# Layer 0's attention: rows normalised two tiles ahead and projected one slot ahead, weight remainders a slot later, and the first steps of the last feed-forward reordered

## The reference

```python
# layer 0, attention: 16 heads of 16; the query is the layer-normalised x
q = (query @ Wq + bq).reshape(B, Nq, H, D).transpose(0, 2, 1, 3)
k, v = (key_value @ Wk + bk), (key_value @ Wv + bv)        # split into heads likewise
attn = jnp.einsum('bhqd,bhkd->bhqk', q, k) * scale
attn = jnp.clip(attn, -CLAMP, CLAMP)
attn = jax.nn.softmax(attn, axis=-1)
x = jnp.einsum('bhqk,bhkd->bqhd', attn, v).reshape(B, Nq, Cq)
return x @ Wo + bo
...
# layer 1, feed-forward: rows and hidden values as 16-bit integers with one scale for the whole tensor
def quantize_a16(x):
    amax = jnp.clip(jnp.max(jnp.abs(x)), 1e-08, None)
    scale = 32767.0 / amax
    x_q = jnp.clip(jnp.round(x * scale), -32768.0, 32767.0) / scale
```

## Time and profile before

| what | us |
|---|---|
| median of three runs | 1161.29 |
| the profiled run's own time | 1163.3 |
| its span, first to last instruction | 1161.2 |
| TensorE (PE) busy | 1057.4 |
| VectorE (DVE) busy | 916.9 |
| ScalarE (ACT) busy | 834.7 |
| GpSimd (POOL) busy | 539.4 |
| layer 0's attention | 0 to about 246 |
| granted TensorE clock, mean | 0.975 |

### The profile page before, as it was taken

One profiled execution on the slowest core, in us unless ns is written; L12 is line 12 of the kernel. 1 busy time (PEld: TensorE's weight loads), 2 busy tenths in 40 slices (PEclk: granted clock), 3 DMA queues, 4 the chain that ended last, 5 costly groups with the idle time before them and its releaser, 6 DMA issues.

```text
span 1161.2 us, 26321 instructions
## 1 busy us (share of the span) xinstructions
PE 1057.4 (91%) x8919; PEld 775.3 (67%) x8919; DVE 916.9 (79%) x1960; ACT 834.7 (72%) x2382; POOL 539.4 (46%) x515
## 2 busy tenths in 40 slices
PE   6888888868969999999999999589999999889898
PEld 5666666645537777777777777357777777645477
DVE  5999999957845687666666667479999999789798
ACT  4988889836656456556556667378888888569896
POOL 5888888732252122122122111178889887500140
PEclk9999999979989999999999999889999999989899
DMA  6443334349672343333333335345252423010034
GB/s 150 118 128 110 110 110 133 123 128 284 189 206 61 53 137 90 118 101 121 124 104 120 121 115 161 112 127 161 68 158 67 154 74 92 28 38 0 1 119 137
DMA packets 128814, 132.12 MB, mean 114 GB/s; under 512 B 24792, under 2 KB 112973, under 8 KB 128557
## 3 DMA queue, kind: packets, MB, share of 16 engines
q1 hardware_dynamic: 119901, 112.17, 32.0%
q0 software_dynamic: 6480, 17.70, 5.5%
q10 hardware_dynamic: 2304, 0.59, 0.3%
HBM read 82.78 MB, written 47.64 MB: 112 GB/s over the span
## 4 chain that ended last, share of the span: by engine, by line
PE 57%; DVE 4%; ACT 4%; issue 2%; DMA 1%; POOL 1%; DVEq 0%; SPq 0%; ACTq 0%; POOLq 0%
PE exp_ps_h L1527 15%; PE exp_ps_y L1540 9%; PE a_ps_o L1953 9%; PE a_ps_sc L1937 8%; PE f_ps_h L2264 5%; PE exp_ps_y L1546 5%; PE a_ps_p L1924 3%; ACT exp_h L1590 2%; DVE f_hlo L2395 2%; PE exp_ps_x L1506 1%; PE f_ps L2447 1%; PE f_ps L2443 1%; PE f_ps_x L2255 1%; DVE all_xn L2404 1%; PE a_ps_x L1911 1%
## 5 line engine op out<-in xcount | busy, mean ns | idle before, releaser
L1590 ACT ACTIVATE exp_h<-exp_ps_h,exp_b_now 128x256 f32<-128x256 f32 (+1 forms) x320 | 124.7, 440 | 142.4 <-PE exp_ps_h L1527 142.4
L1491 POOL DMA_INDIRECT exp_xg<-xn,all_token_of x71 | 84.4, 1188 | 304.0 <-PE exp_ps_x L1506 288.5
L1527 PE MATMUL exp_ps_h<-exp_xhi,exp_w_now 128*128 128x256 bf16 (+1 forms) x1280 | 196.4, 263 | 5.9 <-DVE exp_xlo L1625 5.9
L1986 ACT ACTIVATE a_z<-a_ps_sc,a_nmx 128x77 f32<-128x77 f32 x512 | 159.3, 367 | 35.6 <-DVE a_nmx L2088 35.6
L1527 PE MATMUL exp_ps_h<-exp_xlo,exp_w_now 128*128 128x256 bf16 (+1 forms) x640 | 161.4, 263 | 0.0
L1703 DVE TENSOR_TENSOR exp_hlo<-exp_h,exp_hhi 128x512 bf16<-128x512 f32 (+1 forms) x160 | 99.4, 632 | 70.4 <-ACT exp_hhi L1597 68.5
L1540 PE MATMUL exp_ps_y<-moe_w2s,exp_hhi 128*128 x568 | 134.2, 379 | 1.3 <-DVE exp_y L1722 1.3
L1527 PEld LDWEIGHTS exp_ps_h<-exp_xhi,exp_w_now 128*128 128x128 bf16 x1280 | 120.6, 99 | 20.7 <-issue 8.3
L1986 ACT ACTIVATION_READ_ACCUMULATOR a_z<-a_ps_sc,a_nmx 128x1 f32 x512 | 127.0, 248 | 0.0
L1953 PE MATMUL a_ps_o<-a_v_now,a_phi 128*128 128x256 bf16 (+1 forms) x640 | 106.6, 272 | 2.3 <-DVE a_plo L2077 2.3
L1937 PE MATMUL a_ps_sc<-a_k_now,a_xhi 128*128 128x462 bf16 (+1 forms) x384 | 98.6, 341 | 3.4 <-DMA a_k_now<-fold_klo 2.2
(11 more groups left out here) (279 smaller groups left out, 2735.5 us busy)
## 6 DMA issues: line engine op xcount, KB each, us to landing
a_stage<-in_L_ffn_W_dram SPq DMA_DIRECT2D x64, 256.0 KB, 3.2
y_slots<-exp_y SPq DMA_DIRECT2D x71, 128.0 KB, 1.7
fold_k<-route_kst SPq DMA_DIRECT2D x16, 308.0 KB, 4.5
fold_v<-route_vst SPq DMA_DIRECT2D x16, 308.0 KB
exp_job_in<-fold_k SPq DMA_DIRECT2D x14, 352.0 KB, 3.3
exp_job_in<-fold_v SPq DMA_DIRECT2D x14, 352.0 KB, 3.3
a_x<-in_x_dram SPq DMA_DIRECT2D x32, 128.0 KB, 2.3
x<-a_xo SPq DMA_DIRECT2D x32, 128.0 KB, 1.7
```

What stands on the lines that cost most here:

```text
L1491: pool.indirect_dma_start(out=xg[:, v, u, :], out_offset=None, in_=xn_dram[:, :], in_offset=bass.IndirectOffsetOnAxis(ap=at.bitcast(U32), ...
L1527: mm = pe.matmul(hidden[:, i, f % 2, slots(j)], w1_now[:, v, k, hl, f * P:(f + 1) * P], xx[:, k, slots(j)], start=(q == 0), stop=(q == len ...
L1590: ins = act.activation(h[:, f, slots(j)], hidden[:, i, f % 2, slots(j)], ACT.Gelu_apprx_tanh, bias=b1_now[:, v, f:f + 1])
L1986: ins = act.activation(z[:, u, h * KEYS:(h + 1) * KEYS], ps_sc[:, j, (h - SB[j][0]) * KEYS:(h - SB[j][0] + 1) * KEYS], ACT.Exp, bias=nmx[: ...
```

## The change

In `attention`:

- ScalarE normalises the rows of tile T+2 in slot T (before: T+1), and copies the queries of T+1 (before: T). TensorE starts a slot with the turn of T+1's rows and projects T+1 in the middle of the slot. VectorE copies the turned rows ahead of the maxima. The residual comes after the maxima.
- GpSimd makes the weight remainders of piece T-1 in slot T, ahead of the normalisation of the weights (before: of piece T, one part ahead of and one behind it).
- TensorE's turns and values products alternate: first set of turns, output of T-3, queries of T+1, second set, products of the chunks 0 to 3, third set, products of the chunks 4 to 7, products of the chunks 8 and 9. Each set keeps the order of `turns` among its own.
- ScalarE copies the attended values of T-2 at the end of the slot (before: at the start of the next), and the high parts stand between the copies.
- In slot 0 and 1 the projections of values and keys stand in new places among these.

In `ffn`: the reciprocal of a scale and the per-column steps are computed after the first scaling; `magic` is set in the first phase; TensorE does two products of group 0 ahead of the turns of group 1; the second phase's engines wait for the steps by the first phase's semaphore.

The diff, cut:

```diff
@@ -158,6 +158,7 @@
       if q < ng * LANES and c * P < (q + 1) * PAIR and (c + 1) * P > q * PAIR]
 lanes = [[i for q in range(ng * j, ng * j + ng) for i, (c, qq, _) in enumerate(blocks) if qq == q] for j in range(LANES)]
 turns = [i for row in itertools.zip_longest(*lanes) for i in row if i is not None]
+part = [[i for i in turns if blocks[i][0] // 4 == k] for k in range(3)]
 scale = float(dh) ** -0.5
...
@@ -359,31 +360,32 @@
     def slot(T, t, b):
         u = t % 2
+        v = (t - 1) % 2
+        w1, w2 = split["w1s"], split["w2s"]
+        if has(T - 1):
+            pool.wait_ge(s["hi_done"], 2 * T - 1)
+            at, cols = (T - 1) // 2, slice(v * 512, (v + 1) * 512)
+            pool.tensor_tensor(w1[:, at, 1, cols], stage[:, v, 0, :], w1[:, at, 0, cols],
+                               ALU.subtract).then_inc(s["lo_done"], 1)
         if has(T + 2):
             power(T + 2, u)
+        if has(T - 1):
+            pool.wait_ge(s["hi_done"], 2 * T)
+            pool.tensor_tensor(w2[:, 2 * T - 2:2 * T, D:2 * D],
+                               stage[:, v, 1, :].rearrange("p (g d) -> p g d", d=D),
+                               w2[:, 2 * T - 2:2 * T, 0:D], ALU.subtract).then_inc(s["lo_done"], 1)
         if has(T):
             pool.wait_ge(s["xn_done"], T + 1)
             pool.tensor_tensor(x[:, t, :], x[:, t, :], gbo[:, :], ALU.add).then_inc(s["xb_done"], 1)
-            pool.wait_ge(s["hi_done"], 2 * T + 1)
-            w1, w2 = split["w1s"], split["w2s"]
-            at, cols = T // 2, slice(u * 512, (u + 1) * 512)
-            pool.tensor_tensor(w1[:, at, 1, cols], stage[:, u, 0, :], w1[:, at, 0, cols],
-                               ALU.subtract).then_inc(s["lo_done"], 1)
         if has(T - 1):
-            v = (t - 1) % 2
             pool.wait_ge(s["rsum_done"], T)
             zt = z[:, (T - 1) % NZ, :].rearrange("p (h k) -> p h k", k=KEYS)
             pool.tensor_tensor(zt, zt, rsum[:, v, :].unsqueeze(2).broadcast_to((P, HEADS, KEYS)),
                                ALU.mult).then_inc(s["norm_done"], 1)
-        if has(T):
-            pool.wait_ge(s["hi_done"], 2 * T + 2)
-            pool.tensor_tensor(w2[:, 2 * T:2 * T + 2, D:2 * D],
-                               stage[:, u, 1, :].rearrange("p (g d) -> p g d", d=D),
-                               w2[:, 2 * T:2 * T + 2, 0:D], ALU.subtract).then_inc(s["lo_done"], 1)
     run(pool, slot)
...
@@ -425,24 +426,41 @@
     pe.wait_ge(C.ctx_copied, 2 * B)
     pe.wait_ge(C.ones_row, 1)
     pe.wait_ge(keys_in, 16 * 3)
...
+    def attend(T, some):
+        for i in some:
+            c, q, half = blocks[i]
+            j, g = q // ng, q % ng
+            mine = [cc for cc, qq, _ in blocks if qq == q]
+            n = min(P, ROWS - c * P)
+            mm = pe.matmul(ps_v[32 * j:32 * j + 32, g * P:(g + 1) * P], vblk[0:n, T // TPB % 2, c, half, :], pT[0:n, c, :],
+                           start=(c == mine[0]), stop=(c == mine[-1]))
+        return mm
     keys(0, 1, 0)
     turn_x(0)
     pe.wait_ge(queries_in, 32)
+    queries(0)
     def slot(T, t, b):
...
+        if has(T + 1):
+            wait(pe, s["pT_done"], 3 * (T - 2))
+            pe.wait_ge(s["qT_done"], T + 1)
+            turn_x(T + 1)
         if has(T):
             pe.wait_ge(s["qT_done"], T + 1)
             if t == 0:
...
@@ -454,40 +472,37 @@
                     mm = pe.matmul(ps_sc[:, j, g * PAIR:(g + 1) * PAIR], qT[lane, g, :], kblk[lane, b % 2, g, :],
                                    start=True, stop=True)
             mm.then_inc(s["scores_done"], 1)
+        if T == 1:
+            values(1, 0)
         if has(T - 2):
-            pe.wait_ge(s["norm_done"], T - 1)
             if T == 2:
                 pe.wait_ge(s["kT_done"], 1)
-            for j in range(2):
-                wait(pe, s["pT_done"], 3 * (T - 3) + j + 1)
-                turn_p(T - 2, j)
-            pe.wait_ge(s["qT_done"], min(T + 1, TILES))
-            wait(pe, s["xnT_done"], min(T + 1, TILES))
+            pe.wait_ge(s["norm_done"], T - 1)
+            wait(pe, s["pT_done"], 3 * (T - 3) + 1)
+            turn_p(T - 2, 0)
+        if has(T - 3):
+            output(T - 3)
+        if has(T + 1):
+            queries(T + 1)
+        if has(T - 2):
+            wait(pe, s["pT_done"], 3 * (T - 3) + 2)
+            turn_p(T - 2, 1)
+            wait(pe, s["xo_done"], T - 2)
+            if t == 2:
+                pe.wait_ge(s["v_done"], (T - 2) // TPB + 1)
+            pe.wait_ge(s["pT_done"], 3 * (T - 2) + 1)
+            attend(T - 2, part[0])
+            pe.wait_ge(s["qT_done"], min(T + 2, TILES))
+            wait(pe, s["pT_done"], 3 * (T - 3) + 3)
             turn_p(T - 2, 2)
-        if has(T + 1):
-            turn_x(T + 1)
-        if has(T - 2):
-            wait(pe, s["xo_done"], T - 2)
...
+            pe.wait_ge(s["pT_done"], 3 * (T - 2) + 2)
+            attend(T - 2, part[1])
+            pe.wait_ge(s["pT_done"], 3 * (T - 2) + 3)
+            attend(T - 2, part[2]).then_inc(s["pv_done"], 1)
         if T == 0:
             pe.wait_ge(weights_in, 16 * N_WEIGHTS)
             values(0, 1)
         if T == 1:
-            values(1, 0)
             pe.wait_ge(s["v_rows_done"], 2)
             keys(1, B, 0)
...
-        if has(T - 3):
-            act.wait_ge(s["pv_done"], T - 2)
...
             act.activation(pT[:, 0:4, :].rearrange("p c t -> p (c t)"), ps_p[:, 0, :], ACT.Copy).then_inc(s["pT_done"], 1)
+        if has(T):
+            act.wait_ge(piece_in[u], 32 * (T // 2 + 1))
+            act.activation(split["w1s"][:, T // 2, 0, u * 512:(u + 1) * 512],
+                           stage[:, u, 0, :], ACT.Copy).then_inc(s["hi_done"], 1)
+        if has(T + 1):
+            short_queries(T + 1)
         if has(T - 2):
             act.wait_ge(s["turned_p"], 3 * (T - 2) + 2)
             act.activation(pT[:, 4:8, :].rearrange("p c t -> p (c t)"), ps_p[:, 1, :], ACT.Copy).then_inc(s["pT_done"], 1)
-        if has(T):
-            act.wait_ge(piece_in[u], 32 * (T // 2 + 1))
-            act.activation(split["w1s"][:, T // 2, 0, u * 512:(u + 1) * 512],
-                           stage[:, u, 0, :], ACT.Copy).then_inc(s["hi_done"], 1)
-        if has(T - 2):
             act.wait_ge(s["turned_p"], 3 * (T - 2) + 3)
-            act.wait_ge(s["xnT_done"], min(T + 2, TILES))
             act.activation(pT[:, RCH - 2:RCH, :].rearrange("p c t -> p (c t)"), ps_q, ACT.Copy).then_inc(s["pT_done"], 1)
         if has(T):
             act.activation(split["w2s"][:, 2 * T:2 * T + 2, 0:D],
                            stage[:, u, 1, :].rearrange("p (g d) -> p g d", d=D),
                            ACT.Copy).then_inc(s["hi_done"], 1)
+        if has(T + 2):
+            normal(T + 2, u, (t + 2) % RING)
+        if has(T - 2):
+            act.wait_ge(s["pv_done"], T - 1)
+            wait(act, s["o_done"], T - 2)
+            act.activation(attnT[:, :, :].rearrange("p g t -> p (g t)"), ps_v, ACT.Copy).then_inc(s["attn_done"], 1)
         if T == 0:
             v_copy(0)
         if T == 1:
-            v_copy(1)
             act.wait_ge(s["k_proj"], 2)
             act.activation(kT[:, :, 1:B, :].rearrange("p g b k -> p g (b k)"), ps_p[:, 0:ng, 0:(B - 1) * KEYS],
                            ACT.Copy).then_inc(s["kT_done"], 1)
@@ -653,12 +672,17 @@
             ln_stats(T + 2, u, (t + 2) % RING, b + (t + 2) // RING)
         if has(T + 2):
             ln_mean(T + 2, u)
+        if has(T + 1):
+            turned(T + 1)
         if T == 2:
             block_values(0)
         if t == 3 and b + 1 < B:
             block_keys(b + 1)
         if t == 5 and b + 1 < B:
             block_values(b + 1)
+        if has(T):
+            dve.wait_ge(s["scores_done"], T + 1)
+            dve.tensor_reduce(mx[:, :].rearrange("p (j x) -> p j x", j=LANES), scores, AX, ALU.max).then_inc(s["max_done"], 1)
         if has(T - SKEW):
             v = (t - SKEW) % 2
             turn = b if t >= SKEW else b - 1
@@ -669,11 +693,6 @@
             dve.scalar_tensor_tensor(out=xo[:, v, :], in0=ps_o, scalar=C.gate[:, gate_col:gate_col + 1],
                                      in1=x[:, (t - SKEW) % RING, :], op0=ALU.mult,
                                      op1=ALU.add).then_inc(s["xo_done"], 1)
-        if has(T):
-            dve.wait_ge(s["scores_done"], T + 1)
-            dve.tensor_reduce(mx[:, :].rearrange("p (j x) -> p j x", j=LANES), scores, AX, ALU.max).then_inc(s["max_done"], 1)
-        if has(T + 1):
-            turned(T + 1)
         if has(T + 2):
             ln_shift(T + 2, u)
         if has(T - 1):
...
-def steps_of(dve, sem, count, amax_all, out, tmp):
-    for ins in (lambda: dve.tensor_scalar(tmp[:, 0:1], amax_all[:, 0:1], 1e-8, None, ALU.max),
-                lambda: dve.reciprocal(tmp[:, 1:2], tmp[:, 0:1]),
-                lambda: dve.tensor_scalar(out[:, 0:1], tmp[:, 1:2], 32767.0, None, ALU.mult),
-                lambda: dve.reciprocal(out[:, 1:2], out[:, 0:1])):
-        ins().then_inc(sem, 1)
```

(33 more changed lines are left out.)

90 lines of the change are left out of this document (34 added, 56 removed).

## The result

The changed kernel takes 1163.55 us (median of 20 runs, 1161.00 to 1166.85), the kernel before 1160.99 (20 runs beside it): ratio 1.0022, 95% interval 1.0015 to 1.0028, so 2.6 us slower. I had forecast 1165.8, slower by 4.5. Side and range were right.

What follows compares the result with a forecast made beforehand. VectorE was taken to bound the kernel before (6.81 us a slot), TensorE the changed one (6.95). Slots +2.3, start +1.0, end +2.2 and last stage -1.0 gave +4.5: 1165.8 us, range 1153 to 1171.

Steps and rivals of the forecast that it cites:

- What bounds the kernel now: Layer 0's attention: VectorE sets the 6.81 us slot, 0.50 of it a clamp stall beside GpSimd; real need 6.31.
- Rival C: VectorE stays the bound in layer 0's attention, slots of 6.35 to 6.4, 1147 us; chance 0.12.
- Remainders at nothing: GpSimd's later weight remainders cost nothing and free the clamp (0.50 us); ScalarE stalling on a weight piece would contradict cover.
- The values product: TensorE in layer 0's attention: three parts take 0.88, 1.10 and 0.66, together 2.64 us, against 1.10 of pure work interleaved.
- Rival D: No overlap of TensorE's product parts, full price of passages: slots of 7.2, on average 7.25, 1173 us; chance 0.13.
- TensorE's sum: TensorE's work per changed attention slot: 7.03 to 7.23 us without overlap, 6.5 to 7.1 with it, taken as 6.95.
- Masks: Block masks on VectorE, one of 1.5 us in four slots, cost about 0.05 us a slot on average after the change.
- End: End of layer 0's attention: later output product, split products and later last ReLU, less VectorE's lead, together +2.2 us.
- Start: Start of layer 0's attention: value projections later, first value mask 1 to 1.5 us later, clamp gives 0.4 back: +1.0 us.
- Last stage: Feed-forward: first phase gains 0.34 us and 0.6 us, second phase gains nothing; together -1.0 us.
- A: The forecast case: TensorE bounds layer 0's attention at about 6.95 us a slot, 1163 to 1169 us; chance 0.45.
- B: Deep overlap of product parts two and three (their 20 instructions in 1.3 us): TensorE 6.6, 1155.7 to 1160; chance 0.30.

Runs made afterwards that it cites:

- remainders_later: The kernel before with only GpSimd's two weight remainders of piece T-1 taken in slot T: 1159.4 us, ratio 0.9969 to the kernel before.
- copies_rows_first: The changed kernel with the values product interleaved in one place, ScalarE's copies and rows moved earlier, GpSimd's first ffn scaling behind VectorE's: 1153.09 us, ratio 0.9918.
- together: The changed kernel with the values product as one interleaved list behind all three sets of turns: 1157.59 us, ratio 0.9966 to the kernel before.
- grouped: The kernel of together, with the 34 product instructions in that one place ordered part by part instead of interleaved: 1162.79 us, ratio 1.0009 to the kernel before.
- rows_before_high: The changed kernel with ScalarE's normalised rows of tile T+2 ahead of the second weight piece's high part: 1161.98 us, ratio 0.9993 to the kernel before.
- loop_alone: The kernel before with only ScalarE's third copy of turned probabilities ahead of the first weight high part: 1168.62 us, ratio 1.0057.

## Why the prediction was right or wrong

*What bounds the kernel now: wrong.* I read "VectorE never waits for another engine" in the earlier trace rows as "VectorE's instructions are the period", and took the 0.50 us of stall for a part of its need that could be had. But an instruction that is held up by another engine hides a wait as busy time. remainders_later took the stall away and left 6.82. The ring of ScalarE and TensorE could have been added up from timelines of the kernel before: TensorE's two brackets in the earlier trace rows (0.61 and 0.17, both waiting for a copy of ScalarE) say that TensorE waits for ScalarE, and VectorE's gapless row says nothing on whether it is early. I never asked what ScalarE's queries copy waits for. Rival C touched a ring of this kind, in the changed kernel only.

*VectorE's need of 6.31: about right.* In copies_rows_first's slots of 6.22 VectorE doesn't wait. ScalarE has no gap there either, so they show that VectorE needs 6.22 or less.

*Remainders at nothing: nearly right, but the sign that I had named against it did show.* The clamp fell to 0.11. ScalarE waited for a weight piece four times in the changed kernel, 1.3 us in all, and most of its slots stayed at 6.86 all the same; why those pieces are late is open (see together).

*The values product: the mechanism right, the size 0.3 off.* The part that decides was named: together undoes it alone and gives 0.9966, grouped restores the order alone and gives 1.0009. Part one was forecast at 0.88 + 0.13 = 1.01 and took 0.99. Parts two and three were 1.10 + 0.66 + 0.13 = 1.89 without overlap and took 1.46 (rows_before_high), so they overlap by 0.43. I had bounded the overlap by 0.11 and 0.5 and chosen by "nearer to the shallow end"; it was near the deep one. The forecast of 6.95 left 6.95 - 4.06 = 2.89 for products and passages; measured were 0.99 + 1.46 and 0.15 more in the last two turns (0.37 from start to start for 0.22), 2.60. With no overlap from part to part it would have been 1.89 for parts two and three, and 2.77 for grouped's 34, which took 1.93. Rival D fell with that.

The Trainium skill says in "TensorE: Matmul & The Clock Gate", part 3, that matmuls keep strict program order in start and end. I took that as "nothing overlaps", which is more than it says: by it part three may start as soon as part two's last instruction has started, which saves one round of 0.11 us, and parts two and three would take 1.78. The trace doesn't agree with that either. In the changed kernel part three's six instructions, all of one column group, start at 81.57, 81.71, 81.82, 81.93, 82.03 and 82.15, the last two being the 80-row ones, while those of part two's long group still start every 0.11 us until 81.89. I assign the starts to groups by this spacing; the trace doesn't name the group.

*TensorE's sum.* Measured without a wait 6.70 (rows_before_high), forecast 6.95 with 6.5 to 7.1 as bounds. What I missed is the 0.18 in which the row turns wait for ScalarE: "TensorE without a gap" was not what the profile shows. So 6.86, a tenth below the forecast, is two errors that cancel in part.

*Masks: half right.* I charged 0.05 us a slot for them; they cost next to nothing in the changed kernel (7.28 + 6.43 and 7.63 + 6.19 for two slots of 6.86), while in the kernel before they cost 0.6 and 1.0 each. 29 slots at 6.845 instead of the forecast 7.00 are 4.5 us; that is the term that was mis-sized, from +2.3 to -2.3.

*End: right.* +2.3 for +2.2, the same in all three profiles of the changed attention. *Start: open.* The pair of profiles gives +0.7 for +1.0, and the first value mask 2.2 us later (28.77 for 26.55) where I had 1 to 1.5. But over all thirteen profiles z of tile 2 begins at 32.5 on average with the changed order of TensorE and ScalarE (seven, 31.67 to 33.78) and at 32.3 with the old one (six, 31.88 to 33.01), and the first value mask at 28.2 against 27.4. So the mask comes 0.9 later, and of the +1.0 at z the runs show 0.2, which their scatter doesn't tell from nothing.

*Last stage: wrong.* First phase -0.7 over the runs, for -0.9. In the second I wrote "nothing gained" and left out what the moved release does: GpSimd no longer waits for the magic constant behind VectorE's queue but starts together with VectorE, and VectorE's scaling doubles. +1.44 for 0. It is the same sort of contention, an instruction of VectorE held up by one of GpSimd, that I had read in the clamp at the head of the argument.

In sum: slots 4.6 us better than forecast, last stage 2.2 worse, the rest within the scatter of the stages between, and so 2.6 us slower where 4.5 was forecast. That the number came so near is in part luck: two terms missed by more than the 1.9 us that were left over, in opposite directions. Of the cases, A's own range held the time, but the sign that I had given for B is the one that was seen (the 20 instructions of parts two and three in 1.46 - 0.13 = 1.33 us), and its period with passages at 0.1 to 0.2 (6.6 to 6.8) holds the measured 6.70. B's time was missed by the wait for the rows (3.4 us by rows_before_high) and the last stage (2.2).

## What to carry to other kernels

An engine without gaps isn't the bound until you have checked that nothing in its rows is a wait in disguise: an instruction that takes longer than its like elsewhere is one. Add up every ring that comes back to itself in a slot, across engines, with the weight copies that stand inside it; where two are within 0.1 us of each other, plan to cut both, since either cut alone gives ordinary slots nothing, or harms (here +6.7 us for the first ring alone, -3.6 for the second alone, all of it outside ordinary slots, and -14.6 together). Interleave products over column groups, and when a wait is moved, ask which engines it held apart.

## What the runs showed of the hardware

- TensorE instructions into different 32-column groups run beside one another, though not without limit: the same 34 took 1.41 us interleaved (together), 1.93 part by part in one place (grouped), and 0.99 + 1.46 in two (rows_before_high). One group's own instructions start 0.11 us apart.
- VectorE's 16-column clamp ended with the subtraction of GpSimd that had begun before it: it took 0.61 us where GpSimd had begun 0.58 earlier, 1.02 where it had begun 0.17 earlier (loop_alone), and 0.11 with nothing beside it (remainders_later).
- VectorE's 128x1536 scaling took 2.48 us when GpSimd's like instruction began 0.15 ahead of it, and 1.28 when GpSimd's began 0.19 behind it or after it. Who begins first decides who is held up: GpSimd's took 1.55 in the first case and 1.97 in the second.
